# A two-layer transformer kernel on one Trainium2 core: other orders at the phase starts and ends, and TensorE's buffers at multiples of 256 bytes

## The reference

```python
x = x + mlstm(layernorm(x), ctx, ctx, Wi, bi, Wf, bf, ln_scale)    # 16 heads of 32, gates from x and ctx
x = x + ffn(layernorm(x), ...)      # router, 2 of 8 experts of width 256, plus a shared one of 256
x = x + cross_attention(layernorm(x), ctx, ...)   # 16 heads of 128, rms-normed q and k
x = x + linear(x, ternary(weight)) + bias
```

## Time and profile before

| | |
|---|---|
| Runs | 1341.27, 1344.85, 1345.71 us |
| Profiled execution, its own time | 1339.19 us |
| Its span | 1337.5 us |
| Mean granted clock of TensorE | 0.987 |
| Busy share: TensorE, weight loads, VectorE, ScalarE, POOL | 96%, 79%, 63%, 55%, 28% |
| DMA | 277 MB, mean 207 GB/s |

### The profile page before, as it was taken

How to read it: one execution, slowest core, us unless ns; L and a number is a source line. 1 busy time by engine, 2 the same in 40 slices (tenths; PEclk the granted TensorE clock), 3 DMA queues, 4 the chain that set the end, 5 groups by cost and what they waited for, 6 DMA issues and landing times. The chain is left out here.

```text
span 1337.5 us, 24404 instructions
## 1 busy us (share of the span) xinstructions
PE 1280.8 (96%) x7358; PEld 1059.6 (79%) x7359; DVE 845.0 (63%) x1613; ACT 741.4 (55%) x1831; POOL 379.8 (28%) x353
## 2 busy tenths in 40 slices
PE   7999998999999899899999989999989999999998
PEld 6787776777777678688876778878888888988886
DVE  3545547779778963544445477553587777777965
ACT  5235448788886431454455454545785565565551
POOL 0111015273736026499131342154010000000041
PEclk9999999999999899899999999999999999999999
DMA  7896499787764484666459776564375555555403
GB/s 253 308 366 244 149 310 351 260 292 243 269 218 164 127 318 172 219 205 196 133 186 318 230 264 192 159 203 182 134 221 167 164 153 164 162 161 157 119 27 126
DMA packets 166599, 277.06 MB, mean 207 GB/s; under 512 B 29744, under 2 KB 58160, under 8 KB 166256
## 3 DMA queue, kind: packets, MB, share of 16 engines
q1 hardware_dynamic: 140704, 220.50, 51.1%
q0 software_dynamic: 8672, 29.37, 6.6%
q10 hardware_dynamic: 17136, 26.09, 5.2%
HBM read 167.11 MB, written 108.80 MB: 206 GB/s over the span
## 5 line engine op out<-in xcount | busy, mean ns | idle before, releaser
L3003 ACT ACTIVATE prob<-banks,attend_row,rq 128x128 f32<-128x128 f32 x248 | 110.5, 470 | 0.0
L3016 ACT ACTIVATE attend_ol<-banks,of_attend_vbias 128x512 fp32r<-128x512 f32 x64 | 44.2, 691 | 116.8 <-PE banks L3215 116.8
L121 PE MATMUL banks<-of_shared_split,key_lead 128*128 128x512 f32 x256 | 104.8, 409 | 4.0 <-DVE key_trail L1422 3.8
L121 PE MATMUL banks<-wo,attend_ol 128*128 (+1 forms) x256 | 106.2, 415 | 0.0
L121 PE MATMUL banks<-queries_rows_split,queries_wl 128*128 128x512 f32 x256 | 100.8, 394 | 0.0
L123 PE MATMUL banks<-wo,attend_ot 128*128 (+1 forms) x256 | 100.7, 393 | 0.0
L123 PE MATMUL banks<-of_shared_split,key_trail 128*128 128x512 f32 x256 | 100.6, 393 | 0.0
L122 PE MATMUL banks<-of_shared_split,key_lead 128*128 128x512 f32 x256 | 100.2, 391 | 0.0
L122 PE MATMUL banks<-wo,attend_ol 128*128 (+1 forms) x256 | 99.9, 390 | 0.0
L123 PE MATMUL banks<-queries_rows_split,queries_wt 128*128 128x512 f32 x256 | 99.8, 390 | 0.0
L122 PE MATMUL banks<-queries_rows_split,queries_wl 128*128 128x512 f32 x256 | 99.8, 390 | 0.0
(11 more groups left out here) (399 smaller groups left out, 3522.0 us busy)
## 6 DMA issues: line engine op xcount, KB each, us to landing
mlstm_gmax<-running_max SPq DMA_DIRECT2D x32, 512.0 KB, 6.1
k_heads<-heads_key ACTq DMA_DIRECT2D x64, 256.0 KB, 4.6
q_heads<-queries_head SPq DMA_DIRECT2D x64, 256.0 KB, 2.7
q_ahead<-q_heads SPq DMA_DIRECT2D x64, 256.0 KB, 4.2
of_attend_k<-k_heads SPq DMA_DIRECT2D x60, 256.0 KB, 4.0
of_attend_v<-v_heads SPq DMA_DIRECT2D x60, 256.0 KB, 3.2
key_raw<-in_L_xattn_ki_w SPq DMA_DIRECT2D x20, 512.0 KB, 4.8
sorted_rows<-of_shared_split SPq DMA_DIRECT2D x2, 5120.0 KB, 27.5
```

Source lines behind the costliest of these rows:

```text
L121: nc.tensor.matmul(out, lead_l, lead_r, start=first, stop=False)
L3003: ins = nc.scalar.activation(prob[:, j % 2, b, :], ps[:, j % 2, b * S:(b + 1) * S], ACT.Exp, bias=row[:, j % 2, 1, b:b + 1], scale=rq[:, b ...
L3016: nc.scalar.activation(ol[:, par, j, :], ps[:, 4 + j % 2, :], ACT.Identity, bias=vbias[:, bass.ds(quad_of(it) * 4 + j, 1)]).then_inc(ol_do ...
```

## The change

It has these parts.

1. Addresses. The constants above and four paddings ("line") shift the buffers that TensorE reads to multiples of 256 bytes. No size of any of them changes; the order of two small ones in the shared phase does.
2. Front. The setup phase and its barrier are gone; its instructions stand at the head of POOL's list, and TensorE waits for `made`. Group 0 of the context comes in four column pieces, each followed by its weight piece. TensorE does 10 transposes of the identity (`keep_busy`), then turns 0 and 1, chunk 0, turn 2, chunk 1, turn 3, chunk 2, turns 4 to 7, chunk 3. The cut of the weight trails of quarter 1 starts one unit later.
3. Opening of the heads. VectorE does context sums 0 and 1, `decayed` 0, sums 2 and 3, `decayed` 1 to 3, then the loop.
4. End of the heads. 12 of the 16 token sums stand between the last four key units, the others ahead of tail unit 2. POOL multiplies the last outputs by `lnb` (four operations of 512 columns, in the middle of its weight cut), VectorE multiplies the result by the factor, in reversed order, and adds two of four sequences to x; POOL adds the other two. ScalarE keeps tail unit 2 behind its root.
5. Routed experts. The lead and trail of tile 1 stand ahead of the cut of expert 1; expert 2 goes to POOL, load and cut. Hidden tiles have four pairs of buffers in place of two, and the leads and trails of tiles 0 to 3 stand ahead of the cut of the down weights. 8 transposes of the identity stand behind the first turn.
6. Queries. Late unit 7 stands ahead of the first turn; unit 0 waits for each chunk of the split rows by itself; 14 transposes of the identity stand at the end of the phase.

```diff
-PARKED = 146144
+PARKED = 146432
-TAIL_W, TAIL_V = 119328, 193568
-WO, Q_AHEAD = 129760, 195296
+TAIL_W, TAIL_V = 119552, 193792
+WO, Q_AHEAD = 130048, 195584
-X_LEAD, X_TRAIL = 115232, 59712
-KEY_RAW, KEY_SPLIT = 160288, 195104
+X_LEAD, X_TRAIL = 115456, 59712
+KEY_RAW, KEY_SPLIT = 160512, 195328
+def keep_busy(nc, bank, ident, n):
+    for _ in range(n):
+        nc.tensor.transpose(bank[:, 0:P], ident[:], ident[:])
...
-        TRAILS = {OPENS[q + 1] - (6 if q < QUADS - 2 else 5) + c: (q + 1, c) for q in range(QUADS - 1) for c in range(C)}
+        TRAILS = {OPENS[q + 1] - (6 if 0 < q < QUADS - 2 else 5) + c: (q + 1, c) for q in range(QUADS - 1) for c in range(C)}
...
-            load_ctx(0)
             for c in range(C):
+                sp.dma_start(stage[0][:, :, c * P:(c + 1) * P],
+                             a["ctx_2048"][0:GB, :, c * P:(c + 1) * P].rearrange("b s d -> s b d")).then_inc(ctx_first[c], 16)
                 sp.dma_start(raw[:, c, :], w_dram[c * P:(c + 1) * P, 0:N]).then_inc(first_loaded[c], 16)
             load_ctx(1)
...
-            for t in range(C):
-                turn(t)
+            pe.wait_ge(made, 1)
+            keep_busy(nc, ps[:, 0, :], K.ident, 10)
+            turn(0)
+            turn(1)
             for c in range(C):
                 first_chunk(c)
-                if c < C - 1:
-                    turn(C + c)
+                if c + 2 < C:
+                    turn(c + 2)
                 if c == C - 2:
-                    turn(C + c + 1)
+                    for t in range(C, 2 * C):
+                        turn(t)
...
+                if k == 2:
+                    pool.wait_ge(centred, G)
+                    pool.wait_ge(pv, G * QUADS)
+                    for b in range(GB):
+                        ins = nc.gpsimd.tensor_tensor(cmat[:, b].rearrange("p b s -> p (b s)"),
+                                                      piece(raw_heads(G - 1), b).rearrange("p h e -> p (h e)"), lnb[:], ALU.mult)
+                    ins.then_inc(weighed, 1)
...
+            pool.wait_ge(late_scaled, 1)
+            for b in range(2, GB):
+                xb = K.x[:, (G - 1) * GB + b, :]
+                nc.gpsimd.tensor_tensor(xb, xb, piece(sq, b).rearrange("p h e -> p (h e)"), ALU.add).then_inc(late_added, 1)
...
-            for b in range(GB):
-                context_sum(0, b)
+            context_sum(0, 0)
+            context_sum(0, 1)
             decayed(0, 0, True)
+            context_sum(0, 2)
+            context_sum(0, 3)
+            for n in range(1, 4):
+                decayed(0, n, True)
...
-            for b in range(GB):
+            dve.wait_ge(weighed, 1)
+            for b in reversed(range(GB)):
...
-            own(nc.vector.tensor_tensor(out, out, lnb[:].unsqueeze(1).broadcast_to([P, GB, D]), ALU.mult))
-            xg = K.x[:, last * GB:, :]
-            own(nc.vector.tensor_tensor(xg, xg, out, ALU.add))
+            xg = K.x[:, last * GB:last * GB + 2, :]
+            own(nc.vector.tensor_tensor(xg, xg, out[:, 0:2], ALU.add))
             for b in range(last * GB, B):
+                if b - last * GB >= 2:
+                    dve.wait_ge(late_added, b - last * GB - 1)
                 row_stats.batch(b)
...
+            pe.wait_ge(total_done, CLOSES[G - 2] + 1)
+            pe.wait_ge(c_done, UNITS)
             for m in range(PER - LAG, PER):
                 keys(G - 1, m)
+                token_sums(range(3 * (m - PER + LAG), 3 * (m - PER + LAG) + 3))
...
-    FIRST_EXPERTS = 3
+    FIRST_EXPERTS = 2
...
+        H_DEEP = 4
+        more = sb("more", [P, 2, FC, P], F32R)
+        spare = trail[:, 1].rearrange("p c s -> p (c s)").rearrange("p (m f s) -> p m f s", m=2, f=FC)
...
+            lead_of((0, 1))
             cut_gate_up(1)
             slots(act, slot)
...
+            hidden_lead((0, 0))
+            hidden_lead((0, 1))
+            keep_hidden(move(LAST, -1))
+            silu(LAST)
+            store_hidden(move(LAST, -1))
             act.wait_ge(gu, TILES)
+            hidden_lead((0, 2))
+            hidden_lead((0, 3))
...
             turn_rows((0, 0))
+            keep_busy(nc, ps[:, 6, :], K.ident, 8)
...
-        BEFORE_TURN = 7
+        BEFORE_TURN = 8
...
-                if u < FIRST_HEADS * G and h == 0:
+                if 0 < u < FIRST_HEADS * G and h == 0:
                     pe.wait_ge(trail_done, (g + 1) * C)
...
+                    if u == 0:
+                        pe.wait_ge(trail_done, c + 1)
...
+            keep_busy(nc, ps[:, 7, :], K.ident, 14)
```

109 lines of the change are left out of this document (57 added, 52 removed).

## The result

The changed kernel takes 1330.65 us (median of 4, 1328.61 to 1332.38), the kernel before in the same session 1343.94 (1341.27 to 1345.71). The ratio is 0.9898, with a 95% interval of 0.9882 to 0.9915: 13.3 us faster, where 17.8 were forecast and 1311 to 1338 was the range. The two traces are one execution each: that of before stood 4.75 under its median of 1343.94, this one 1.73 over its own, and 6.81 + 4.75 + 1.73 = 13.3. So two traces tell where steps went, but not their whole sum.

What follows compares the result with a forecast made beforehand. TensorE was taken as the bound, busy 1280.8 of 1337.5 us, so edits gain only by ending its idle or altering time per matmul. Terms 1.2 + 1.6 + 2.0 + 2.2 + 3.2 + 3.2 + 3.7 + 0.7 = 17.8 give 1327.0; range 1311 to 1338.

Steps and rivals of the forecast that it cites:

- its own signs: Wrong if named steps differ over 1 ns, new stops over 1 us follow, or VectorE waits for POOL's adds.
- Front: Start of kernel: chunk 0 at about 7.4, 3.5 us sooner, 1.2 kept (0 to 2.7); later weight cut 1.6 more.
- Rival (c): First 250 us: DMA, not order, sets the time; front, opening and end-of-heads gains lost, 1332; 0.18 together with (e).
- Opening of the heads: Scores near 200.8, keys resumed at 203.2, 3.5 us sooner, part handed back: 2.0 us gain (0 to 3.5).
- End of the heads: 3.4 us leave VectorE's chain for POOL; 2.2 us gain taken, 0.5 of it from the clock (0 to 3.5).
- Routed start: Start of the routed stage: tile 1 2.5 sooner, or 3.7 at full clock; 3.2 us gain (2.5 to 4.8).
- Down stage: Turn to the down stage: tile 4 at 692.1 for 695.4, 3.2 us gain (2 to 5.5); nothing in 35 tiles behind.
- Queries: Start of queries: late unit 7 fills the stop, unit 0 goes chunk by chunk; 3.7 us gain (2.5 to 4.2).
- End of queries: 14 transposes fill 1.5 of 2.9 us of barrier, attend opening need not run low; 0.7 us gain (0 to 1.7).
- Addresses: 512-column matmuls in all phases: zero gain taken, bounds about -11 us to +27; called the largest unknown.
- rival (b): 512-column matmuls everywhere: pace falls to 226.7 ns with the new addresses, 1316 us; chance 0.16.
- Rival (d): Filling transposes don't hold the clock at front, end of heads, routed start, end of queries: 3.4 us less, 1330.4; chance 0.12.

## Why the prediction was right or wrong

The sign, the range and the rough size are right; 13.3 of 17.8 us came. That the sum came so near is in part luck: two steps failed outright and lost some 5 us together where 4.2 us of gain were forecast, and the routed start, the down stage and the addresses gave more than forecast. No lower bound lay below 0, although both failed steps moved work beside other work that it could hold up. By its own signs, too, the prediction is wrong in part: new stops of over 1 us stand at three of the places (of_ffn_raw 1.2, key_trail 2.4, heads_total 8.0), the stop before tile 4 of the down stage is still 2.2, and stretches at 0.50 are left from 212.7, 444.8, 482.4, 694.0 and 967.1 on. (Its upper bounds sum to 27.5, not 27.6.) By its steps:

**Front.** Of the "1.2 of the 3.5" that I meant to keep nothing is shown: the kernel with the old front reached the heads 2.6 us sooner than before, as early as any but two of the twelve with the new one; this is the bound of 0. Rival (c) has the result, transfers that set the pace; what the traces show is a wait for ScalarE's copy, of 1.2 to 1.5 us. The landmarks were placed well: first matmul 6.86 (7.4 forecast), the copy of unit 0 at 22.62 (23), no wait for of_ctx_trail.

**Opening of the heads.** This step failed. The second scores came 2.1 us sooner, as forecast, but "part is handed back" was more than all: a loss of 1.9 to 3.4 us. I had put the lower bound at 0. The evidence was near, in the rows I quoted, DMA at 1.02 of its time. What I missed is that a store issued 0.7 us later can land 2 us later, and that ScalarE's next copy needs its buffer.

**End of the heads.** This step failed as well: 2.2 forecast, and instead the phase ends 3.9 to 5.9 us later than before, again past its lower bound. To the first routed transpose it is about 3, with the 1.7 to 1.9 of the addresses already taken off. I costed VectorE's operations by rows in which POOL stood. Where they start within a POOL operation, those that took 0.68 us take up to 1.74, since they end 0.55 behind POOL's; VectorE's list got 1.85 us longer in place of 3.4 shorter, and the addition that TensorE's sums wait for is one of the held ones. And I moved the sums without asking what stands behind their wait on TensorE's queue: tail unit 2, 12 matmuls on the lower clock.
The Trainium skill, "GPSIMD Engine Reference", Specifications, says that GpSimd shares its SBUF interfaces with VectorE and that instructions of VectorE with two SBUF inputs contend. The held rows are all of this kind, and a reduction with one input keeps its 1.19 us within POOL's multiply (431.19 in the changed kernel, 432.20 with the old end), so the traces agree.

**Routed start.** 3.2 forecast, 4.3 to 5.4 measured, the upper bound being 4.8. From the phase's first transpose tile 1 starts 3.8 us sooner (7.67 for 11.45), the 3.7 of my better case, and tile 2 another 1.1 (11.58 for 16.46): the term mis-sized is what I took off because tile 2 would be late next. Expert 2 on POOL costs nothing, as forecast.

**Down stage.** 3.2 forecast, 4.4 measured. The turn gave 2.9, the same in every trace (tile 4 starts 8.63 us behind the last gate-and-up matmul, for 11.51). The other 1.5 stand in the 35 tiles behind; 1 us of it is likely the depth of the buffers, which I had written off because ht was ready before the small stops.

**Queries.** 3.7 forecast, 3.6 measured. **End of queries.** 0.7 forecast, nothing measured (0.1 us longer): the barrier's wait is 1.4 us for 2.9, as the transposes fill it, and the clock falls behind it in most traces.

**Addresses.** Zero forecast, -1.7 to -1.9 measured. The value lies well inside the bounds, and on the side of rival (b), but only where the pace was 233 ns; groups at 229 to 231 ns stayed there. The Trainium skill, "Advanced Engine Details and Errata", Memory Cachelines, says that SBUF has 16-byte lines and that accesses within one line run at full performance. Read as I read it, that gives no gain at all; the measurement decides against this reading for two groups of products.

**Rival (d).** The Trainium skill's rule that transposes don't count as busy ("TensorE: Matmul & The Clock Gate", Part 4) doesn't hold for these float32 transposes, which the profile lists as MATMUL: 36 of them alone stood ahead of the clock's return from 0.50 to 1.00 at the end of the heads, 6.8 us behind its fall, where it is 10.2 in the same kernel without them. Yet rival (d) is near in time: the 1.2 and 0.7 us that I gave to the clock at the routed start and the end of the queries weren't there to be had.

## What to carry to other kernels

Before moving work to an idle engine, look for rows in which both engines already run side by side; here two-input operations of VectorE ended only behind POOL's, and the trace of before had rows that say so; and before moving a wait, read what is queued behind it. When a step is made earlier in a stretch where DMA is full, cost what it sets free to be transferred, not only what it needs. Here two of eight steps lost more than they won, and the sum hid it. Compare stages between landmarks over several executions, as two traces of these kernels can differ by more than any one part is worth. And follow a gain to the next landmark: a clock kept up, or a phase ended sooner, was spent on the next wait three times here.

## What the runs showed that I had not expected

The clock falls while TensorE does matmuls of one column, which the profile counts as busy (32 in 4.29 us, 0.50 from 444.0 on), and transposes placed behind them then cost twice their time. VectorE's small operations suffer most beside POOL: 1.28 us for 0.22 in one (L1207, the variances' product, 64 columns), which ends 0.08 us behind POOL's operation. Moving the buffers up to multiples of 256 bytes took 6.6 of 233.3 ns from a matmul in two groups and nothing that can be seen from the others.
